# One change to a memory-learning, attention and expert kernel: first weights filled by GpSimd, unused TensorE products in its waits, the last step formed as a mean

## Chip, cores and metric

The kernel runs on one core of one Trainium2 chip, as one program in a single launch. The metric is its device time in microseconds (us), the median of three runs. A profiled execution of the same program gives the rows below. TensorE, VectorE, ScalarE, GpSimd and SyncE stand in the profile as PE (PEld for its weight loads), DVE, ACT, POOL and SP.

## What is computed

Input x is 4 x 32 x 32 x 128 in float32: 4 batches, 32 steps, 32 rows of 128 features. Three layers follow each other, each with a residual sum:

```python
# 1. a small two-block MLP (W1 128x256, W2 256x128, twice) learns per batch by momentum over 32 steps
k, v = l2norm(x_t @ Wk), x_t @ Wv                  # x group-normalised
g = grad(mean((mlp(params, k) - v)**2))            # per batch
mom = eta * mom - lr * g                           # eta, lr, forget: per batch and step
params = params * (1 - forget) + mom
final = mean over the batches of params            # after the last step
x = x + mlp(final, l2norm(x @ Wq))
# 2. banded additive attention over 1024 tokens (32 keys each): tanh(q + k), softmax, weighted sum
# 3. eight experts, the best two per token: softmax router, layernorm, gelu MLP 128-512-128
```

Only the mean of the learned weights is read after the last step, not the weights of each batch.

## The kernel before

The program is five blocks, one after another, each with an instruction stream per engine written out by hand and semaphores between them; at a block's end all engines meet.

- `prepare` loads and normalises x, projects it (8 steps at a time, `CH`), and leaves the normalised keys (`ktok`, and turned `kf`), the scaled values `vs`, the turned queries `qf` and the gates `coef`. VectorE's L255 writes the normalised input `xg`; every projection on TensorE (L180) waits for all four parts. At its end VectorE (L287) and GpSimd (L219) each scale half of `vs`, behind GpSimd's last difference (L216), and VectorE copies the last two blocks of turned queries (L260). ScalarE's queue issues the loads of the first weights (`first10` to `first21`, L94 and L96, semaphore `load_p`); ScalarE waits for them at its end.
- `learn` is the 32 steps. W, M (momentum) and KW (kept part of W) are tiles of 128 x (4 batches x 256) for each of the four weights "10", "20", "11", "21"; WT are turned copies of W. The loop is rotated (`rotated`): a forward for step 0, then 31 turns of backward(t) and forward(t), then backward and the rest of step 31. Ahead of it ScalarE (L528) and VectorE (L630) copy the first weights four times each, and GpSimd clears M (L448) before it copies the coefficients of step 0 (L405). In a step ScalarE makes KW (L483, `keep_of`), the Gelus (L456) and copies out of PSUM; TensorE makes each gradient per batch (`grad_1`, `grad_2`, L669 and L676) into four PSUM banks; VectorE folds them into M (L541, `momentum`); GpSimd (L384, `add`) and for "20" VectorE (L550) sum KW and M to the new W. Layer 10's gradient comes last, behind L579 of the step. SyncE fills the expert rows in HBM by DMA (L372, L373), behind three small fills (`pad_ready`).
- `read_out` reduces W over the batches on VectorE (L959, then L961), in the order 10, 20, 11, 21, and runs the MLP over 8 tiles of 512 tokens: TensorE L905, L915, L925, L935, ScalarE the Gelus, VectorE the sums, statistics and the normalisation `xl` (L966), which waits for `rstd` from GpSimd (`root`, L840 and L842). GpSimd's stream has the conversion of the eight experts' weights into two bfloat16 parts first (L850 to L856), with root(0) ahead of the last one and root(1) behind them.
- `attend` sums and squashes query and key bands (VectorE L1060, ScalarE L1087), sums over units on TensorE, and makes the first softmax. Its last TensorE work is 8 turns (L1127); VectorE's softmax of the first two tiles runs behind it.
- `experts` starts with the routing: for 8 token tiles TensorE turns the attention weights (`weights`, L1378) and applies them (`values`, L1386 and L1388). For each group of two tiles (four groups, `GR`) VectorE normalises (L1540), `router` turns the tokens (L1399) and makes the logits (L1405), VectorE picks two experts, `counts` (L1412, L1413) ranks them, VectorE writes `place` (L1592), and GpSimd sends 16 scatters of rows to HBM (L1361). When all have landed SyncE loads the rows of each job (39 jobs of 256 rows), TensorE turns (L1434) and multiplies them (L1461, L1476), and the results are scattered, gathered and summed (L1702).

The order inside an engine is the order of the code, for instance TensorE's in the routing:

```python
                for n in range(2):
                    weights(n)
                    values(n)
                for g in range(GR):
                    if 2 * g + 2 < NTB:
                        weights(2 * g + 2)
                        values(2 * g + 2)
                    router(g)
                    if 2 * g + 3 < NTB:
                        weights(2 * g + 3)
                        values(2 * g + 3)
                    counts(g)
```

## Time and profile before

| | |
|---|---|
| three runs | 984.9, 987.91, 993.33 us; median 987.91 |
| the profiled execution | 990.18 us, its span 988.3 |
| mean granted TensorE clock | 0.884 of full |
| busy in the span | PE 790.3 us, DVE 731.2, ACT 617.9, POOL 615.3 |
| stages (us from the span's start) | prepare to 72, learning to 575, read-out to 654, attention to 709, routing to 828, experts to 960, sum of the results to the end |

The page shows the span in 40 slices of 24.7 us, with the busy tenths of each engine and the granted clock (9 is 90% or more, 5 is half). A timeline row is start, length, engine, line, operation, output and inputs; several alike in a row are merged (x8), the bracket tells how long the engine had been idle and who released it. The length of one product on TensorE has its drain in it; the distance of two starts is what it costs in a stream.

### The profile page before, as it was taken

The numbers are of one execution on the slowest core, as the hardware profiler recorded it, in microseconds if no ns is written. First come the engines' busy times: TensorE is split into PE (matmuls) and PEld (weight loads), VectorE is DVE, ScalarE is ACT, GpSimd is POOL, SyncE is SP. The second block draws the span as 40 slices with busy tenths as digits, with TensorE's granted clock in tenths as the row PEclk, the third lists the DMA queues.
The fourth block names the chain that finished last, engine by engine and source line by source line (L and its number), as shares of the span: only waits on it lengthen the run. The fifth ranks groups of instructions, "written<-read, shape, count | busy, mean of one in ns | idle before, by whom it ended". The sixth has DMA issues, their size and how long they took to land. (4 is left out here: it accounts for less than half of the span.)

```text
span 988.3 us, 24782 instructions
## 1 busy us (share of the span) xinstructions
PE 790.3 (80%) x7837; PEld 501.2 (51%) x7837; DVE 731.2 (74%) x1853; ACT 617.9 (63%) x1382; POOL 615.3 (62%) x759
## 2 busy tenths in 40 slices
PE   2957999999999999999999969946565522999960
PEld 2544555555555555555555524421254421899950
DVE  4485888888888888888888852759677770777747
ACT  3756877777778777777787713239533421888840
POOL 0145878878788788787887859710006774466660
PEclk8988999999999999999999969968855555999985
DMA  7009999990000000000000032032001112233318
GB/s 231 1 2 206 160 202 147 10 5 0 0 0 0 0 0 0 0 0 0 0 0 0 1 87 86 0 102 89 2 1 43 50 52 57 75 90 91 95 50 254
DMA packets 105404, 54.07 MB, mean 55 GB/s; under 512 B 42624, under 2 KB 96664, under 8 KB 105360
## 3 DMA queue, kind: packets, MB, share of 16 engines
q1 hardware_dynamic: 98976, 43.34, 27.8%
q0 software_dynamic: 4544, 9.38, 2.9%
q10 hardware_dynamic: 1840, 0.79, 0.3%
q8 instruction: 24, 0.39, 0.2%
q14 instruction: 20, 0.16, 0.1%
HBM read 21.49 MB, written 29.44 MB: 52 GB/s over the span
## 5 line engine op out<-in xcount | busy, mean ns | idle before, releaser
L384 POOL TENSOR_TENSOR s_w<-l_kw,l_m 128x512 f32<-128x512 f32 x192 | 260.0, 1355 | 15.4 <-DVE l_m L541 9.9
L541 DVE SCALAR_TENSOR_TENSOR l_m<-l_m,l_eta,lp_g 128x256 f32<-128x256 f32 x512 | 225.0, 477 | 26.5 <-PE lp_g L676 20.2
L483 ACT ACTIVATE l_kw<-s_w,l_keep_lr 128x256 f32<-128x256 f32 x384 | 173.7, 505 | 19.1 <-POOL l_keep_lr L405 19.1
L1366 POOL DMA_INDIRECT f_yg<-f_yr,f_xmeta x78 | 78.4, 1005 | 54.5 <-DVE f_yr L1696 41.7
L1361 POOL DMA_INDIRECT f_xg<-f_xrow,f_place x64 | 63.0, 985 | 54.8 <-DVE f_place L1592 36.2
L389 POOL TENSOR_TENSOR l_kw<-s_w,l_keep 128x512 f32<-128x512 f32 x64 | 71.9, 1124 | 0.0
L1341 ACT ACTIVATE f_hh<-fp_v,f_bcol 128x256 f32<-128x256 f32 x156 | 61.2, 476 | 13.1 <-PE fp_v L1461 9.3
L477 ACT COPY l_wt<-lp_b 128x512 f32<-128x512 f32 x96 | 56.4, 588 | 15.5 <-PE lp_b L662 15.5
L662 PE MATMUL lp_b<-s_cst,s_w 128*128 128x128 f32 x384 | 62.2, 285 | 0.7 <-ACT s_w L528 0.7
L1461 PE MATMUL fp_v<-f_xf,s_w_hi 128*128 128x256 bf16 x312 | 54.6, 277 | 2.3 <-DVE f_xmeta L1676 1.9
L650 PE MATMUL lp_h<-s_w,l_gf 128*32 128x128 f32 x1024 | 41.7, 280 | 18.2 <-ACT l_gf L470 18.2
L662 PEld LDWEIGHTS lp_b<-s_cst,s_w 128*128 128x128 f32 x384 | 43.3, 142 | 24.3 <-DVE l_gp L573 13.2
L550 DVE TENSOR_TENSOR s_w<-l_kw,l_m 128x512 f32<-128x512 f32 x64 | 49.5, 773 | 1.2
L1687 DVE TENSOR_TENSOR f_hs_lo<-f_hh,f_hs_hi 128x512 bf16<-128x512 f32 x52 | 33.6, 689 | 21.4 <-ACT f_hs_hi L1347 21.4
L676 PE MATMUL lp_g<-l_dh,l_g 32*128 32x128 f32 x512 | 45.7, 296 | 0.0
L669 PE MATMUL lp_g<-l_da,l_h 32*128 32x256 f32 x256 | 44.9, 427 | 0.0
L1060 DVE TENSOR_TENSOR t_h<-s_qp,s_kp 128x1056 f32<-128x1056 f32 x32 | 37.5, 1255 | 9.9 <-ACT s_kp L1083 9.9
L216 POOL TENSOR_TENSOR proj<-s_ktok,proj 128x1024 f32<-128x1024 f32 x4 | 8.8, 2191 | 55.6 <-DVE s_ktok L276 55.6
L650 PEld LDWEIGHTS lp_h<-s_w,l_gf 128*32 128x32 f32 x1024 | 25.3, 110 | 35.5 <-issue 25.3
L1461 PE MATMUL fp_v<-f_xf,s_w_lo 128*128 128x256 bf16 x156 | 43.2, 277 | 0.0
L676 PEld LDWEIGHTS lp_g<-l_dh,l_g 32*128 32x128 f32 x512 | 33.5, 185 | 16.8 <-DVE l_m L541 12.3
L662 PE MATMUL lp_a<-s_cst,s_w 128*128 128x128 f32 x256 | 42.0, 287 | 0.0
(320 smaller groups left out, 2029.8 us busy)
## 6 DMA issues: line engine op xcount, KB each, us to landing
f_xg<-s_pad SPq DMA_DIRECT2D x1, 17280.0 KB, 107.8
f_xt<-f_xg SPq DMA_DIRECT2D x39, 130.0 KB
r_w<-in_L_ffn_W_dram SPq DMA_DIRECT2D x16, 256.0 KB, 3.2
s_w<-f_yg SPq DMA_DIRECT2D x16, 256.0 KB, 3.7
xs<-in_x_dram SPq DMA_DIRECT2D x4, 512.0 KB, 6.8
t_w<-in_L_ffn_W_dram SPq DMA_DIRECT2D x8, 256.0 KB
out_dram<-s_x SPq DMA_DIRECT2D x8, 256.0 KB, 3.1
s_xsh<-s_xl SPq DMA_DIRECT2D x4, 448.0 KB, 3.5
```

The source lines that it names most:

```text
L384: nc.gpsimd.tensor_tensor(W[k][:, half(h), :], KW[k][:, half(h), :], M[k][:, half(h), :], ALU.add).then_inc(w_ready[k], 1)
L389: nc.gpsimd.tensor_tensor(KW[k][:, half(h), :], W[k][:, half(h), :], keep[:, half(h)].rearrange("p (b a) -> p b a", a=1).to_broadcast([128 ...
L477: nc.scalar.copy(flat(WT[k][:, half(h), :]), wt_bank(k, h)).then_inc(wt_ready, 1)
L483: m = nc.scalar.mul(KW[k][:, b, :], W[k][:, b, :], keep_lr[:, b:b + 1])
L541: i = nc.vector.scalar_tensor_tensor(out=M[k][:, b, :], in0=M[k][:, b, :], scalar=eta[:, b:b + 1], in1=ps_g[b][:, 0:256], op0=ALU.mult, op ...
L650: i = nc.tensor.matmul(p[rows(b), 0:128], x[:, 128 * h + 32 * b:128 * h + 32 * b + 32], w[:, b, 128 * h:128 * h + 128], start=h == 0, stop ...
L662: i = nc.tensor.transpose(wt_bank(k, h)[:, 128 * j:128 * j + 128], W[k][:, 2 * h + j // 2, 128 * (j % 2):128 * (j % 2) + 128], ident)
L676: i = nc.tensor.matmul(ps_g[b][:, 128 * h:128 * h + 128], x[rows(b), 128 * h:128 * h + 128], y[rows(b), :], start=True, stop=True)
L1341: nc.scalar.activation(hh[j % 2][:, h, :], ps_h[j % 2][:, SL * h:SL * h + SL], ACT.Gelu, bias=bcol[:, h, j:j + 1]).then_inc(h_ready, 1)
L1361: nc.gpsimd.indirect_dma_start(sb["xg"][:, :], bass.IndirectOffsetOnAxis(ap=place[:, g, k, i:i + 1], axis=0), row[k][:, tile_of(g, i), :], ...
L1366: nc.gpsimd.indirect_dma_start(sb["yg"][:, :], bass.IndirectOffsetOnAxis(ap=xmeta[:, j, a, 0:1].bitcast(mybir.dt.int32), axis=0), yr[j % R ...
L1461: m = nc.tensor.matmul(p, chosen(w1s[b], e, h), xf[j % 2][:, c, :], start=r == 0, stop=r == 2)
```

## The change

First, the weights of the first step are filled by GpSimd in `prepare`, when `load_p` has come. The value product is cut at 24 of 32 steps between VectorE and ScalarE (GpSimd has none), and ScalarE copies the last block of turned queries. GpSimd's clearing of M and the two fills for SyncE's DMA stand behind the first forward.

```diff
@@ prepare
+                act.wait_ge(coef_ready, 1)
+                act.wait_ge(k_pad_v, NCK + 1)
+                for t in range(T - CH, T):
+                    nc.scalar.mul(sb["vs"][:, t, :], proj[:, t, 256:384], sb["coef"][:, t, 8:9])
+                act.wait_ge(qk_turned, 4 * NCK - 1)
+                nc.scalar.copy(q_block(2 * NCK - 1), ps[5][:, :].rearrange("p (t b c) -> p t b c", t=4, b=B))
...
+                pool.wait_ge(load_p, 16 * 4)
+                for k in PARAMS:
+                    nc.gpsimd.tensor_copy(sb["w" + k][:, :, :], sb["first" + k][:, :].rearrange("p (a n) -> p a n", a=1).to_broadcast([128, B, 256]))
...
-                pool.wait_ge(k_pad_v, NCK + 1)
-                pool.wait_ge(coef_ready, 1)
-                nc.gpsimd.tensor_tensor(sb["vs"][:, T // 2:T, :], proj[:, T // 2:T, 256:384], sb["coef"][:, T // 2:T, 8:9].to_broadcast([128, T // 2, 128]), ALU.mult)
...
-                dve.wait_ge(k_pad_v, NCK + 1)
-
-                nc.vector.tensor_tensor(sb["vs"][:, 0:T // 2, :], proj[:, 0:T // 2, 256:384], sb["coef"][:, 0:T // 2, 8:9].to_broadcast([128, T // 2, 128]), ALU.mult)
-                for g in range(2 * NCK - 2, 2 * NCK):
-                    q_turned(g)
+                dve.wait_ge(k_pad_v, NCK)
+                nc.vector.tensor_tensor(sb["vs"][:, 0:T - CH, :], proj[:, 0:T - CH, 256:384], sb["coef"][:, 0:T - CH, 8:9].to_broadcast([128, T - CH, 128]), ALU.mult)
+                q_turned(2 * NCK - 2)
```

GpSimd's stream from prepare to the loop of learning, before (`s_kf` keys, `l_m` M, `l_kw` KW, `l_keep_lr` coefficients, `s_padrow` the fill for the DMA):

```order
L212 MEMSET s_kf 128x128
L216 ISA
L216 TENSOR_TENSOR proj<-s_ktok,proj 128x8x128 x4
L219 TENSOR_TENSOR s_vs<-proj,s_coef 128x2048
L76 UNCONDITIONAL_BRANCH
L375 UNCONDITIONAL_BRANCH
L442 MEMSET l_none 128x4
L443 MEMSET s_padrow 128x270
L444 IOTA s_padrow 128x270
L445 COPY l_kt<-s_kf 128x128
L448 MEMSET l_m 128x512 x8
L405 COPY l_keep_lr<-s_coef 128x5
```

And now, where M lies in `s_w_mem` and KW in `s_xsh` (the rows from L80 to L456 are in learning):

```order
L231 COPY s_w<-s_first 128x1024 x4
L235 ISA
L235 TENSOR_TENSOR proj<-s_ktok,proj 128x8x128 x4
L80 UNCONDITIONAL_BRANCH
L389 UNCONDITIONAL_BRANCH
L459 MEMSET l_none 128x1 x4
L418 COPY l_keep_lr<-s_coef 128x5
L420 TENSOR_TENSOR l_keep<-l_keep_lr,l_none 128x4
```

Four copies of 1024 elements stand ahead of the first difference, the product of L219 is gone, and the eight fills (now L454) come behind eight further instructions of the first forward.

Second, the last step has functions of its own (`last`). Gradients are made for the sum of the batches, in one product over all 128 rows, where `grad_1` and `grad_2` made one for each batch; no W is formed. For "10" the sum over the batches of eta M + KW and the gradient are added in one PSUM bank, and ScalarE scales it; for the others VectorE adds the gradient to batch 0's decayed M, and `read_out` sums M and KW over the batches:

```diff
@@ learn
+                def total(t, k, n):
...
+                    nc.vector.scalar_tensor_tensor(out=M[k][:, 0, :], in0=M[k][:, 0, :], scalar=eta[:, 0:1],
+                                                   in1=ps_g[n - 1][:, 0:256], op0=ALU.mult, op1=ALU.add).then_inc(decayed_ready, 1)
...
+                    total(t, "21", 1)
+                    slope_times(t, 1, ps_a, DG1)
+                    decayed(t, "10", (0, 1))
+                    decayed(t, "10", (2, 3))
+                    dve.wait_ge(mm_done, t * 7 + DH1)
+                    nc.vector.tensor_tensor(dh1[:, :], ps_h[:, 0:128], dp[:, :], ALU.add).then_inc(chain, 1)
...
+                    act.wait_ge(grad_done, t * 6 + 4)
+                    nc.scalar.mul(sb["wf"]["10"][:, :], ps_g[3][:, 0:256], 1.0 / B)
...
+                    pe.wait_ge(decayed_ready, 5)
+                    for b in range(B):
+                        nc.tensor.matmul(ps_g[3][:, 0:256], ident, M["10"][:, b, :], start=b == 0, stop=False)
+                    pe.wait_ge(kc_ready, t + 1)
+                    pe.wait_ge(chain, t * 6 + K_DA0)
+                    total_1(ps_g[3], kc, da[0], start=False)
@@ read_out
+                    if e == 0:
+                        pool.wait_ge(wf_ready, len(PARAMS) - 1)
...
+                n = mean(0, "20", ())
+                n = mean(n, "11", (1, 2, 3))
+                mean(n, "21", (1, 2, 3))
```

TensorE's end of learning, from the product with the turned "11" on, before (`lp_g` gradient banks, `l_dh` and `l_da` the errors, `l_kc` the keys):

```order
L650 MATMUL lp_h<-l_wt,l_daf 32x128 x8
L669 MATMUL lp_g<-l_da,l_h 128x256 x2
L656 MATMUL lp_t<-s_cst,l_dh 128x128
L676 MATMUL lp_g<-l_dh,l_g 128x128 x4
L642 MATMUL lp_b<-l_wt,l_dh1f 32x256 x4
L676 MATMUL lp_g<-l_dh,l_g 128x128 x4
L669 MATMUL lp_g<-l_da,l_kc 128x256 x4
```

And now:

```order
L707 MATMUL lp_h<-l_wt,l_daf 32x128 x8
L713 MATMUL lp_t<-s_cst,l_dh 128x128
L818 MATMUL lp_g<-l_dh,l_g 128x128 x2
L699 MATMUL lp_b<-l_wt,l_dh1f 32x256 x4
L851 MATMUL lp_g<-s_w_mem,s_cst 128x256 x4
L813 MATMUL lp_g<-l_da,l_kc 128x256
```

The gradients by batch are one or two products each, and four with the identity (`s_cst`) stand ahead of the last. M, KW and eta now outlive `learn`: they lie in the space of `w2_both` and `xsh`.

Third, products whose result nobody reads: 3 and 2 in `prepare` (float32, 384 columns), 26 at the end of `attend`, and in `experts` 4 ahead of each values' wait, 5 and 3 in `router`, 8 ahead of the wait in `counts`, 4 and then 16 ahead of a group, 76 ahead of turn(0) (bfloat16, 384 columns):

```diff
+def unused(nc, sb, p, n):
+
+    w = sb["w1_hi"]
+    for _ in range(n):
+        nc.tensor.matmul(p[:, 0:384], w[:, 0, 0:128], w[:, 1, 0:384], start=True, stop=True)
@@ experts
                 def values(n):
+                    unused(nc, sb, ps_xn, 4)
                     pe.wait_ge(at_ready, n + 1)
...
                 m.then_inc(table_done, 1)
+                unused(nc, sb, ps_am, 76)
                 turn(0)
```

TensorE's stream of group 0, from its first router work to the ranks, before (`fp_x`, `fp_y`, `fp_v` PSUM, `f_xn` tokens, `f_am` attention weights):

```order
L1399 MATMUL fp_x<-s_cst,f_xn 128x128 x8
L1405 MATMUL fp_y<-f_wr,f_xnf 128x8 x8
L1378 MATMUL fp_y<-s_cst,f_am 128x128 x4
L1379 MATMUL fp_x<-s_cst,f_tail 128x128
L1386 MATMUL fp_v<-s_xsh,f_at 128x128 x4
L1388 MATMUL fp_v<-s_xtail,f_at 128x128 x4
L1412 MATMUL fp_y<-f_both,s_cst 128x64
```

And now:

```order
L1118 MATMUL fp_y<-s_w_hi 128x384 x5
L1521 MATMUL fp_x<-s_cst,f_xn 128x128 x4
L1118 MATMUL fp_y<-s_w_hi 128x384 x3
L1521 MATMUL fp_x<-s_cst,f_xn 128x128 x4
L1527 MATMUL fp_y<-f_wr,f_xnf 128x8 x8
L1496 MATMUL fp_y<-s_cst,f_am 128x128 x4
L1497 MATMUL fp_x<-s_cst,f_tail 128x128
L1118 MATMUL fp_x<-s_w_hi 128x384 x4
L1505 MATMUL fp_v<-s_xsh,f_at 128x128 x4
L1507 MATMUL fp_v<-s_xtail,f_at 128x128 x4
L1118 MATMUL fp_y<-s_w_hi 128x384 x8
L1535 MATMUL fp_y<-f_both,s_cst 128x64
```

Nothing of the real work has moved; L1118 stands in front of what waits.

## Rows read from the trace of the kernel before

**Rows 1.** The page's 40 slices: the granted clock, in tenths of full.

```profile
PEclk8988999999999999999999969968855555999985
```

**Rows 2.** Timeline of the start of learning, and the same Gelus in the loop.

```profile
72.69 1.28 ACT L524 ACT_TABLE_LOAD   x1 [4.09 <-PEq L76]
...
73.74 4.63 POOL L448 MEMSET l_m<- 128x512 f32 x8
...
79.01 0.36 ACT L456 ACTIVATE l_g<-lp_a 128x256 f32<-128x256 f32 x1
...
84.58 0.38 ACT L456 ACTIVATE l_g<-lp_b 128x256 f32<-128x256 f32 x1
...
554.50 0.38 ACT L456 ACTIVATE l_g<-lp_a 128x256 f32<-128x256 f32 x1 [0.78 <-PE lp_a L689]
...
558.82 0.38 ACT L456 ACTIVATE l_g<-lp_b 128x256 f32<-128x256 f32 x1
```

**Rows 3.** Timeline of the end of prepare.

```profile
65.42 3.64 POOL L219 TENSOR_TENSOR s_vs<-proj,s_coef 128x2048 f32<-128x2048 f32 x1
...
65.45 5.76 DVE L287 TENSOR_TENSOR s_vs<-proj,s_coef 128x2048 f32<-128x2048 f32 x1 [1.47 <-POOL proj L216]
...
71.13 1.27 DVE L260 COPY s_qf<-pp 128x512 f32<-128x512 f32 x2
```

**Rows 4.** Timeline of the last step and the start of the read-out.

```profile
566.89 0.64 PE L642 MATMUL lp_b<-l_wt,l_dh1f 128*32 128x256 f32 x8
...
572.18 2.48 POOL L384 TENSOR_TENSOR s_w<-l_kw,l_m 128x512 f32<-128x512 f32 x2 [2.13 <-DVE l_m L541]
...
577.28 3.78 PE L905 MATMUL rp_a<-s_qf,r_wf 128*128 128x512 f32 x4 [6.24 <-DVE r_wf L961]
...
590.95 1.88 PE L925 MATMUL rp_a<-r_h,r_wf 128*128 128x512 f32 x4
```

**Rows 5.** GpSimd's timeline: the first scatters of groups 0, 1 and 2.

```profile
743.11 1.29 POOL L1361 DMA_INDIRECT f_xg<-f_xrow,f_place  x1 [32.91 <-DVE f_place L1592]
...
764.87 0.96 POOL L1361 DMA_INDIRECT f_xg<-f_xrow,f_place  x1 [1.02 <-DVE f_place L1592]
...
787.42 0.95 POOL L1361 DMA_INDIRECT f_xg<-f_xrow,f_place  x1 [2.29 <-DVE f_place L1592]
```

**Rows 6.** The tile of the first weights (its loads, all landings), then VectorE's timeline.

```profile
L96 ACTq DMA_DIRECT2D s_first<-in_L_conv_w_dram x2: 468/482/497, 6.4 to 6.9; - x2
DMA to landing us min/median/max: 13.4/13.9/14.5
...
21.79 2.98 DVE L255 TENSOR_SCALAR xg<-s_vs,grs,gneg 128x1024 f32<-128x1024 f32 x4
```

**Rows 7.** Timeline of the read-out: GpSimd's root(1) and its user.

```profile
629.19 1.04 POOL L842 TENSOR_TENSOR r_rstd<-r_ve,r_mhalf 128x4 f32<-128x4 f32 x1
...
631.71 1.91 DVE L966 TENSOR_SCALAR s_xl<-s_x,s_mv,r_rstd 128x128 f32<-128x128 f32 x4
```

**Rows 8.** The chain at the start of the experts' products.

```profile
834.96 1.47 PE fp_v L1461 x6
...
844.88 1.31 PE fp_v L1461 x12
```

**Rows 9.** Windows: length, busy (x) of PE, PEld, DVE, ACT, POOL, clock, DMA, GB/s.

```profile
690.00:700.00 10.00, 5.53 (x36) 1.25 (x36) 9.73 (x9) 9.01 (x10) 0.00 (x0) 1.00 0.00 0
710.00:720.00 10.00, 6.90 (x33) 5.65 (x34) 8.50 (x28) 2.35 (x5) 0.20 (x1) 0.50 0.04 6
743.10:764.90 21.80, 14.62 (x70) 12.27 (x70) 15.80 (x71) 8.51 (x12) 16.21 (x17) 0.50 0.15 49
```

**Rows 10.** The chain from 709.6 to 743.2, then TensorE's timeline at 723.

```profile
by line: PE fp_v L1386 12.4%; PE fp_y L1405 9.6%; PE fp_y L1378 9.2%; DVE f_am L1501 7.7%; PE fp_x L1399 6.7%; DVE f_xn L1540 5.8%; ACT f_xrow L1316 5.3%; ACT f_at L1293 5.2%; PE fp_v L1388 4.5%; issue 3.7%; ACT L1320 3.4%; DVE f_bst L1512 
718.50 2.08 PE fp_v L1386 x8
...
723.35 1.16 PE L1386 MATMUL fp_v<-s_xsh,f_at 128*128 128x128 f32 x8 [0.84 <-ACT f_at L1294]
```

345 lines of the change are left out of this document (212 added, 133 removed).

## Prediction

> **What bounds the kernel now.** I read the page's slices first, then the timeline at the places that the diff touches, then windows, the chain and GpSimd's own timeline in the routing. In the slices [rows 1] TensorE's granted clock is at half (5, of its two levels of 2.4 and 1.2 GHz the lower) around slice 28 to 33, at about 0.8 twice before that, and at full elsewhere. The 31 turns of the learning loop in the middle have the same instructions in both kernels (only addresses and buffers differ), so I put their change at 0 and look at six seams.
>
> At the start of learning [rows 2] the Gelu of step 0 begins at 79.01, 6.32 us after the block's first instruction at 72.69: ScalarE's first kept weights wait for the coefficients that GpSimd copies behind 4.63 us of memsets. From that Gelu to the second one takes 5.57 us (79.01 to 84.58), in the loop 4.32 (554.50 to 558.82), though the loop also does gradients there: TensorE starts at half clock. At the end of prepare [rows 3] VectorE's product of 2048 elements shows 5.76 us. GpSimd's equal product ran from 65.42 to 69.06, and VectorE ended at 71.21, 2.15 us later, which is what 2048 elements cost it. So it stood still while GpSimd had the memory, and both must end before learning begins. At the end of learning [rows 4] the last backward product is done at 567.5, but GpSimd's last sums of weights end at 574.66 and the first product of the read-out starts at 577.28, at half clock. In the routing GpSimd scatters rows in 4 groups of 16; it starts each group when VectorE has placed it, and once going it idles only 1.02 and 2.29 us before groups 1 and 2 [rows 5].
>
> **The change part by part.** *Weights filled in prepare.* GpSimd copies four tiles of 1024 elements. A copy isn't in the trace; its memset takes 4.63/8 = 0.58 per 512 elements [rows 2], its sum with two inputs 1.24 [rows 4], so one tile costs 1.2 to 2.5, and I take 1.2 (one input, like the memset), 4.6 in all. They wait for the loads issued at 6.4 to 6.9, which land 13.4 to 14.5 later, so they begin at about 20.5, and VectorE makes the normalised input at 21.79 to 24.77, all of which TensorE waits for [rows 6]. If VectorE stands still as at 65.45, the copies left at 21.8 (3.3 us) stand in front or between. Some of VectorE's small steps before fall beside them, so +2.8; bounds 0 and +4.8 (all four, none beside).
> The Trainium skill says the same of such pairs ("SBUF — State Buffer", Who interferes with whom): a VectorE copy or tensor_scalar in a two-port mode, or an instruction with two inputs in SBUF, and a reading GpSimd instruction shut each other out for the whole instruction. Row 65.45 agrees with it (3.6 us of standstill). By the rule 4.8 is the most it could cost, without it the term would be 0 and the sum 2.8 lower.
>
> *End of prepare.* The value product is cut anew: VectorE does 24 steps (3072 elements, 3.2 us by 2.15 for 2048) and GpSimd none, ScalarE does 8 small ones and one turned block. VectorE no longer waits for GpSimd's last difference but can't run beside it, which ended at 65.45 [rows 3]: 65.45 + 3.2 + one copy of 0.64 = 69.3, against 71.13 + 1.27 = 72.4: -3.1. ScalarE's new eight of some 0.2 to 0.4 us (estimated from the 0.36 of its 256-element Gelu in [rows 2]) and the copy follow its last turned keys and end at about 69 to 70.5. The unused products keep the clock there. I take -3.0, bounds 0 and -4.
>
> *Start of learning.* The copies of weights (8 on ScalarE, 8 on VectorE) and the copy of the keys are gone, and GpSimd's memsets stand behind its first pass. Gelu then waits for ScalarE alone: table load 1.28, a one-column Gelu 0.2, one kept product 0.45: 1.95 instead of 6.32, -4.4. With at most a microsecond or two between TensorE's unused products and its first real ones, it starts at full clock: -1.2 (5.57 to 4.32). The memsets now end about 9.2 us into the block, and TensorE's first gradient product of the loop waits for them at about 9.0: +0.3. The two fills for SyncE's DMA stand behind them; that DMA is wanted at 743 only. Together -5.3, bounds -4 and -6.5.
>
> *Last step.* Gradients are summed over the batches in one product; GpSimd has nothing. VectorE's decayed momenta of layer 10 now stand ahead of its next chain step and wait for ScalarE's kept products: some 0.7 late, so the last backward product ends at about 568.2. Then TensorE does four 256-column sums with the identity and one gradient. Two 512-column products are 4 records and 1.88 in all, 0.43 apart (at 590.95) [rows 4], so one of 256 columns is 0.43, five 2.2, with the drain 570.6, and ScalarE's scaling 0.4: 570.9. The block ends 3.7 earlier than by 574.66. The first read-out product needs nothing more: it starts at about 571.4, not 577.28, and after less than 1 us of idle at full clock, so the first two steps take 1.88, not 3.78 each: at the first product of layer 11 (590.95 before) TensorE is 9.1 ahead. VectorE's three means take 8.2 us from the block's start and are there when wanted.
> But GpSimd converts expert weights from the block's start in both, and normalising tile group 1 waits for a root that it makes behind them. Before, that root was done at 630.23 and used at 631.71 [rows 7], 1.5 of slack. It moves by 3.7 only, so at this point the gain is 3.7 + 1.5 = 5.2. VectorE then finds TensorE's products waiting and catches up about 1.1 in the tail: -6.3. Bounds: -3.7 (block alone) and -9.1 (TensorE alone).
>
> *Attention.* Its body is VectorE's and unchanged. In its last idle stretch 26 unused products of 384 columns run: 12 of 256 take 1.31 at full clock [rows 8], 0.109 each, so 0.164 here, 4.3 in all. Beside them VectorE does the softmax of the first tiles, some 4 us too, so what can reach past the block's end is a little: +0.1, bounds 0 and 0.5 (4 if the clock were at half).
>
> *Routing.* In this stage the clock is 0.50 though TensorE is busy 14.62 of 21.8 us per group, while attention holds it at 1.00 with 5.53 of 10 [rows 9]. The same 8 value products take 2.08 at one level and 1.16 at the other [rows 10]. If the fill keeps the level, the real work of a group is about 7.5 and its 40 unused products (4+4, 5+3, 8, 16) are 6.6: 14 of 20, so they fit in waits. What it buys: up to the first normalised tokens VectorE sets the pace (8.50 of 10 busy), so 0.8 of the 1.5 idle. Behind them the turns of the tokens (L1399, 6.7% of the chain's 33.6 us) and the router's products (L1405, 9.6%) stand on the chain [rows 10], 5.5, half saved, 2.7; a cast of ScalarE's takes back 0.3 and I take 2.5. The first scatter so starts 3.3 earlier than 743.11. From there GpSimd sets the end: 64 scatters of 1.26. A group's period falls from 21.8 to about 19, below its 20.2, so of faster groups only the two idles count, 1.02 + 2.29 less the usual 0.3 each: 2.7. Sum -6.0; if nothing comes of it 0, and at most -9 (if the value products and turns before the first normalised tokens, L1386, L1388 and half of L1378 or 7.2 us, save their half too).
>
> *Start of experts.* The 76 unused products end before the first rows land (12.5 at full clock, up to 25 at half, from about 806) and may leave an idle stretch in which the clock falls again. At full clock the first 6 products take 0.7 instead of 1.47, and from 844.88 on the stage is already at full [rows 8]. -0.4, between 0 and -0.9.
>
> Sum: +2.8 - 3.0 - 5.3 - 6.3 + 0.1 - 6.0 - 0.4 = -18.1. The profiled execution took 990.18, so 972.1; it is 2.3 above the median of the three runs shown (987.91), by which it would be 969.8. I take 971.
>
> **The rivals.** *The unused products become the bound (slower).* For it: the clock stayed at half in the routing at 67% busy. At half a product of 384 columns costs 0.33, 40 of them 13.1, and 14.62 + 13.1 = 27.7 is more than the 21.8 of a group. Groups 1 and 2 then slip by 5.9 and 5.3, the first and last by about 6 together, and the scatters end 16 later; the 76 in front of the first turned rows (25 us) add some 9. +25 against -11.7 elsewhere: 990.2 + 13 = 1003, with the median's offset 1001. It decides once the routing loses more than 12. Against it: TensorE would then be busy all the time with wide products, and such stretches are at full level everywhere else. 5%.
> *The fill holds no clock but fits, and the routing gains nothing.* GpSimd's 64 scatters then start at 743.1 as before: -12 in all, 976. 12%.
> *GpSimd holds both ends.* The copies cost 4.8 and the read-out gains only the 3.7 of the block: +2.0 and +2.6 on the sum, -13.5: 975. 15%. With the rival before: 980 to 981, 8%.
> *It doesn't do what it says.* If the last step's sums cost as much as the old path (VectorE's decays blocking the chain), the seam gives 0 and the sum is -11.8: 976. 5%.
>
> **How the numbers follow.** The forecast has 55%, the rivals 5, 12, 15, 8 and 5. Three runs of the kernel before spread from 984.9 to 993.33, and about 1% (9.9 us) is what tells it from no change: faster is below 978. The forecast, the two cases at 975 and 976 and most of the last give 0.82; the double case and tails of the others 0.13; the half-clock case 0.05. The range reaches from 961 (every term at its good end but one) to 983.
>
> **What would show it.** Right: Gelu of step 0 about 2 us after its block starts; no GpSimd work in the last step, the first read-out product 6 us earlier in its stage and at 1.88; clock 1.00 through 710 to 800, the first scatter some 3 us nearer to the routing's start, scatters without gaps. Wrong: VectorE's normalised input no longer than 2.98 near 21.8; slices of 0.5 in the routing, or TensorE never idle there; gaps between scatter groups; or a loop turn of other length, which times 31 would upset everything.

## The result, and the profile after

The changed kernel takes 974.69 us (median of 4: 972.06, 972.13, 977.25, 977.40), the kernel before, run beside it, 986.72 (984.90 to 993.33). The ratio is 0.9853, with an interval of 0.9821 to 0.9885: faster by about 1.5%. The forecast was 971 with a range of 961 to 983. Its profiled execution took 972.06 with a span of 970.2, against 990.18 and 988.3: 18.1 less, the sum of the forecast, though not by its terms in every place. The two profiled executions flatter the change: the one before lies 3.5 above its median and the one after 2.6 below its own, so the medians differ by 12.0 only. The four times lie in two pairs 5.2 apart, and the profile shows one of the lower pair. The experiments find two things that such a spread can come from; no trace shows the upper pair itself.

From the page of the changed kernel, the granted clock in 40 slices of 24.3 us, in tenths of full:

```profile
PEclk8899999999999999999999999967999867999985
```

The five half-clock slices of [rows 1] (717 to 840 us) are gone. What is left is at the end of the read-out and the attention's start (6, 7), and in the later part of the routing and in front of the experts (8, 6, 7). Windows of 10 us have 1.00 from 670 to 750, then 0.83, 0.95 and 0.84, and from 780 on:

```profile
780.00:790.00 10.00, 0.00 (x0) 0.00 (x0) 9.24 (x26) 0.00 (x0) 7.56 (x9) 0.50 0.14 47
790.00:800.00 10.00, 8.94 (x43) 4.83 (x44) 1.20 (x3) 0.00 (x0) 7.56 (x9) 0.68 0.17 55
```

A row of windows gives the length, then for PE, PEld, DVE, ACT and POOL the busy time and the number of instructions, then the granted clock, the DMA share and GB/s. TensorE's last product of the routing starts at 778.29, so up to 806 the half clock behind it hits only the 76 unused products.

Timeline of VectorE and GpSimd at the first weights, after (start us, busy us, engine, line, operation, and in brackets the idle time before it with what ended it):

```profile
21.10 4.90 POOL L231 COPY s_w<-s_first 128x1024 f32<-128x1024 f32 x4 [20.16 <-DMA s_first<-in_L_conv_w_dram]
...
22.19 5.08 DVE L271 TENSOR_SCALAR xg<-s_vs,grs,gneg 128x1024 f32<-128x1024 f32 x4
```

It answers to [rows 6]: VectorE's four instructions grew from 2.98 to 5.08, and even the four small ones ahead of them (0.16 in all) took 0.60. The first projection product moved from 24.83 to 27.33.

Timeline of the end of prepare and the start of learning, after:

```profile
66.44 4.55 DVE L302 TENSOR_TENSOR s_vs<-proj,s_coef 128x3072 f32<-128x3072 f32 x1
70.92 0.68 DVE L276 COPY s_qf<-pp 128x512 f32<-128x512 f32 x1
...
72.18 1.28 ACT L558 ACT_TABLE_LOAD   x1 [0.25 <-PEq L80]
...
74.12 0.36 ACT L468 ACTIVATE l_g<-lp_a 128x256 f32<-128x256 f32 x1
...
79.36 0.38 ACT L468 ACTIVATE l_g<-lp_b 128x256 f32<-128x256 f32 x1 [0.46 <-PE lp_b L699]
```

Against [rows 2, 3] the table load stands 0.5 earlier although 2.5 were lost in front of it, so the end of prepare gave 3.0. The first Gelu follows 1.94 behind the load instead of 6.32; from it to the second one are 5.24, not the 4.3 of full clock.

Timeline of VectorE and TensorE in the last step and the read-out's start, after:

```profile
558.55 0.88 DVE L658 SCALAR_TENSOR_TENSOR s_w_mem<-s_w_mem,s_eta,s_xsh 128x256 f32<-128x256 f32 x2 [0.76 <-ACT s_xsh L495]
559.35 0.28 DVE L682 TENSOR_TENSOR l_dh<-lp_h,l_dp 128x128 f32<-128x128 f32 x1
...
560.97 1.99 PE L851 MATMUL lp_g<-s_w_mem,s_cst 128*128 128x256 f32 x8
...
564.11 1.96 PE L1001 MATMUL rp_a<-s_qf,s_first 128*128 128x512 f32 x4 [0.72 <-PEq L379]
```

The last forward's second Gelu is at 551.92 (558.82 before [rows 2]), so all in front of it gave 6.9. From there to the first read-out product are 12.19 instead of 18.46 [rows 4], and that product is at full clock.

GpSimd's timeline, a window of the routing of one scatter group's length, and the chain in front of the experts, after:

```profile
725.35 1.29 POOL L1479 DMA_INDIRECT f_xg<-f_xrow,f_place  x1 [28.76 <-DVE f_place L1719]
```

```profile
725.35:746.00 20.65, 15.23 (x115) 10.90 (x116) 17.61 (x76) 8.41 (x12) 15.92 (x16) 1.00 0.15 50
```

```profile
815.40 1.47 PE fp_v L1588 x6
```

The last of the 64 scatters is at 807.56, and none behind the first waited for VectorE, where [rows 5] show two that did. The window is at 1.00 with 115 instructions of TensorE where [rows 9] has 0.50 with 70. The experts' first six products are still at half, 1.47 as in [rows 8].

| stretch | before | after |
|---|---|---|
| to the first projection product | 24.83 | 27.33 |
| to the table load of learning | 47.86 | 44.85 |
| to the second Gelu of step 0 | 11.89 | 7.18 |
| to the same Gelu of step 1 | 17.02 | 15.25 |
| to the same Gelu of step 31 | 457.22 | 457.31 |
| to the read-out's first product | 18.46 | 12.19 |
| to the attention's first product | 77.69 | 77.47 |
| to the first scatter | 88.14 | 83.77 |
| to the last scatter | 83.97 | 82.21 |
| to the first result scatter | 19.97 | 19.94 |
| to the last result scatter | 112.96 | 113.02 |
| to the end of the span | 28.29 | 29.68 |

The table follows the span from mark to mark, in one execution of each kernel ("the same Gelu" is the second Gelu of that step). The experiments are read by it, since a mark in a profile is surer than a few microseconds in a median. Three seams come out nearly alike in all fourteen traces of this study: from the table load to the first Gelu are 6.32 and 6.31 in the kernel before and e2, and 1.94 in the other twelve; from the last step's second Gelu to the read-out's first product are 18.46 and 18.47 in those two and 11.34 to 12.19 in the others; and from the first projection product to the table load 47.86 and 47.69 against 44.5 to 45.8. No experiment takes these three parts of the change out again.

### The profile page after: what moved, and what is told of

Its sections match the earlier page's. It is cut to its first block and busy times, and to the rows that moved or that the text cites. A ratio compares the mean times of both kernels' runs of the same rounds, so it can differ in the third digit from the quotient of the medians.

```text
span 970.2 us, 25223 instructions
## 1 busy us (share of the span) xinstructions
PE 811.6 (84%) x8069; PEld 506.3 (52%) x8069; DVE 722.1 (74%) x1846; ACT 618.1 (64%) x1384; POOL 608.7 (63%) x758
## 3 DMA queue, kind: packets, MB, share of 16 engines
q1 hardware_dynamic: 98976, 43.34, 28.9%
## 5 line engine op out<-in xcount | busy, mean ns | idle before, releaser
L398 POOL TENSOR_TENSOR s_w<-s_xsh,s_w_mem 128x512 f32<-128x512 f32 x186 | 251.8, 1354 | 8.9 <-DVE s_w_mem L570 3.4
L570 DVE SCALAR_TENSOR_TENSOR s_w_mem<-s_w_mem,s_eta,lp_g 128x256 f32<-128x256 f32 x496 | 217.8, 475 | 24.0 <-PE lp_g L733 18.6
L495 ACT ACTIVATE s_xsh<-s_w,l_keep_lr 128x256 f32<-128x256 f32 x384 | 173.8, 505 | 17.5 <-POOL l_keep_lr L418 17.4
L403 POOL TENSOR_TENSOR s_xsh<-s_w,l_keep 128x512 f32<-128x512 f32 x64 | 72.1, 1126 | 0.0
L1459 ACT ACTIVATE f_hh<-fp_v,f_bcol 128x256 f32<-128x256 f32 x156 | 61.1, 476 | 13.1 <-DVE f_hs_lo L1814 5.6
L579 DVE TENSOR_TENSOR s_w<-s_xsh,s_w_mem 128x512 f32<-128x512 f32 x62 | 48.0, 775 | 1.1
L489 ACT COPY l_wt<-lp_a 128x512 f32<-128x512 f32 x64 | 37.7, 589 | 6.8 <-PE lp_a L719 6.8
```

Of the source, the lines that this page charges most:

```text
L398: nc.gpsimd.tensor_tensor(W[k][:, half(h), :], KW[k][:, half(h), :], M[k][:, half(h), :], ALU.add).then_inc(w_ready[k], 1)
L403: nc.gpsimd.tensor_tensor(KW[k][:, half(h), :], W[k][:, half(h), :], keep[:, half(h)].rearrange("p (b a) -> p b a", a=1).to_broadcast([128 ...
L489: nc.scalar.copy(flat(WT[k][:, half(h), :]), wt_bank(k, h)).then_inc(wt_ready, 1)
L495: m = nc.scalar.mul(KW[k][:, b, :], W[k][:, b, :], keep_lr[:, b:b + 1])
L570: i = nc.vector.scalar_tensor_tensor(out=M[k][:, b, :], in0=M[k][:, b, :], scalar=eta[:, b:b + 1], in1=ps_g[b][:, 0:256], op0=ALU.mult, op ...
L1459: nc.scalar.activation(hh[j % 2][:, h, :], ps_h[j % 2][:, SL * h:SL * h + SL], ACT.Gelu, bias=bcol[:, h, j:j + 1]).then_inc(h_ready, 1)
```

## The experiments

Twelve kernels were made for it. Times are medians, and ratios are to the kernel before, run beside each. "Course" is one of two lengths that the same rows of instructions took.

### e1: no unused products behind learning

```diff
 def unused(nc, sb, p, n):
-    w = sb["w1_hi"]
-    for _ in range(n):
-        nc.tensor.matmul(p[:, 0:384], w[:, 0, 0:128], w[:, 1, 0:384], start=True, stop=True)
+    return
```

> The changed kernel without its unused products behind the attention, in the routing and in front of the experts; those in prepare stay. In the changed kernel the first scatter starts 83.97 us after the attention's first product (641.38 to 725.35) and the last one 82.21 behind the first; before it was 88.49 and 83.97. Theory (the fill holds TensorE's clock, and that is the whole of the routing's gain): the clock is at half again in the routing, the two stretches come back to 88.5 and 84.0, and the profiled execution takes 6.3 more than 972.1, so 978.4. Rival (the gain comes from the earlier seams shifting the stage, not from the clock): 84.0 and 82.2 stay, 972. In front of the experts nothing changes by either, since the first products there ran at half clock with the fill too.

980.43 us (976.41 to 981.61), ratio 0.9906 (0.9878 to 0.9934): 5.7 more than the changed kernel, 5.2 by the ratios. A window of one scatter group and GpSimd's scatters, the first and those that waited:

```profile
732.60:754.00 21.40, 14.62 (x70) 12.27 (x70) 15.47 (x69) 8.51 (x12) 16.15 (x16) 0.50 0.15 49
```

```profile
732.59 1.29 POOL L1477 DMA_INDIRECT f_xg<-f_xrow,f_place  x1 [32.41 <-DVE f_place L1717]
...
754.34 0.96 POOL L1477 DMA_INDIRECT f_xg<-f_xrow,f_place  x1 [1.02 <-DVE f_place L1717]
...
776.89 0.96 POOL L1477 DMA_INDIRECT f_xg<-f_xrow,f_place  x1 [2.28 <-DVE f_place L1717]
```

The window at 0.50, the 14.62 busy and both waits of before [rows 5, 9] are back within 0.01. (The attention's first product is at 641.58 and 654.97; the 641.38 of this expectation, and in e4's the 77.27, come from a row of SyncE's just ahead of it, so 83.97 and 88.49 are 83.77 and 88.14.) From the attention's first product to the first scatter are 87.59, and 84.21 to the last. From VectorE's first sum of the attention to the last scatter are 164.84, as in the kernel before (164.89), and 159.42 in the changed kernel. The rival (earlier stages shift this one) falls, and the fill is the gain, through the clock. In front of the experts, 19.91 instead of 19.94 without the 76: they buy nothing. The read-out took 80.57 instead of 77.47 here, though nothing in it was changed; see e5.

### e2: the kernel before with the unused products alone

The edit is the diff's own lines in the attention and the routing, except the 76.

> The kernel before with only the unused products added: 26 behind the attention, 4+4, 5+3, 8 and 16 per group in the routing; none in prepare, none in front of the experts. Theory (the fill works alone): attention's first product to first scatter 84.0 instead of 88.49, first to last scatter 82.2 instead of 83.97, all else as before: 990.2 - 6.3 = 983.9 for a profile like the one of before, ratio 0.994. Rival (the fill pays only together with the other edits, or costs where TensorE is late): less than 3 us of it, ratio 0.997 or above.

984.64 us, ratio 0.9957 (0.9939 to 0.9975): 4.2 less than before. The profile has 82.09 for the scatters as expected, but 86.65 in front of them, and in this execution the fill gave 2.0 in all (162.89 from the attention's first sum to the last scatter). The fill works alone, and gives 4 rather than 6 in the median. Its span, 987.6, also holds a first turn of the loop of 19.21: the stop of 1.38 that the kernel before has there too, and behind it the clock at 0.50 from 98 to 104.

### e3: copies of the first weights later

```diff
                 pool.wait_ge(load_p, 16 * 4)
+                pool.wait_ge(xg_ready, B)
                 for k in PARAMS:
```

> The changed kernel with GpSimd's four copies of the first weights behind VectorE's normalised input instead of beside it. Theory (the two engines shut each other out of the memory): VectorE's four instructions take 2.98 again instead of 5.08, the first projection product moves from 27.33 to about 24.9, and everything behind it by as much: -2.4, 969.7 for the profiled execution. Rival (the lengthening has another cause, such as the loads from DRAM landing then, or the later copies hit the next VectorE work, the norms from some 32 on, as hard): less than 1 us.

971.96 us (970.45 to 975.41), ratio 0.9846 (0.9812 to 0.9880). VectorE's and GpSimd's timelines:

```profile
21.87 2.98 DVE L272 TENSOR_SCALAR xg<-s_vs,grs,gneg 128x1024 f32<-128x1024 f32 x4
...
25.01 3.98 POOL L232 COPY s_w<-s_first 128x1024 f32<-128x1024 f32 x4 [24.06 <-DVE xg L272]
...
34.69 2.29 DVE L283 TENSOR_REDUCE ss<-xs 128x16 f32<-128x2048 f32 x1 [9.84 <-ACT xs L128]
```

2.98 again, the projection at 24.91 and the table load at 69.43 instead of 72.18. Apart, both engines are shorter (3.98 against 4.90 for the copies), and VectorE idles 9.84 behind them anyway. The times of whole runs can't tell 2.4 here; the marks can.

### e4: GpSimd's first two roots earlier

```diff
-                    if e == E - 1:
-                        root(0)
...
                     nc.gpsimd.tensor_copy(sb["w1_hi"][:, e, :], w1g[e % 2][:, :]).then_inc(w_hi, 1)
+                    if e >= E - 2:
+                        root(e - (E - 2))
...
-                root(1)
```

> The changed kernel with GpSimd's first root inside the last expert but one and its second inside the last expert, each ahead of the two subtractions. In the changed kernel VectorE idles 2.48 and 2.56 for them (611.96 and 619.37). Theory (GpSimd holds the read-out from the first normalised group on): both idles shrink below 0.5, the attention's first product comes some 2 to 3 us sooner after the read-out's first one than 77.47 (564.11 to 641.38 is 77.27), 969.5 in all. Rival (TensorE's own row of products is as long, so that it takes the place of the root): under 0.7 us.

971.18 us (968.96 to 972.47), ratio 0.9833 (0.9805 to 0.9861). VectorE's three first normalisings in the changed kernel and in e4:

```profile
611.96 1.69 DVE L1076 TENSOR_SCALAR s_xl<-s_x,s_mv,r_rstd 128x128 f32<-128x128 f32 x4 [2.48 <-POOL r_rstd L937]
...
619.37 2.07 DVE L1076 TENSOR_SCALAR s_xl<-s_x,s_mv,r_rstd 128x128 f32<-128x128 f32 x4 [2.56 <-POOL r_rstd L937]
...
623.74 1.08 DVE L1076 TENSOR_SCALAR s_xl<-s_x,s_mv,r_rstd 128x128 f32<-128x128 f32 x4
```

```profile
610.18 3.22 DVE L1075 TENSOR_SCALAR s_xl<-s_x,s_mv,r_rstd 128x128 f32<-128x128 f32 x4
...
616.48 2.77 DVE L1075 TENSOR_SCALAR s_xl<-s_x,s_mv,r_rstd 128x128 f32<-128x128 f32 x4
...
623.79 1.12 DVE L1075 TENSOR_SCALAR s_xl<-s_x,s_mv,r_rstd 128x128 f32<-128x128 f32 x4 [2.00 <-POOL r_rstd L937]
```

Both waits are gone, but the read-out shortened by 1.4 only (76.07). Counted from its first product, the first group begins 2.4 earlier and ends 0.8 earlier, since the same instructions take 3.22 instead of 1.69 beside GpSimd's subtractions; the second ends 2.8 earlier; and the third begins only 0.5 earlier, because it now waits 2.00 for the third root, which stands behind the clears. So GpSimd held the read-out by three things in turn: its order, its work beside VectorE's, and the clears.

### e5: SyncE's large DMA early again

```diff
                 for k in PARAMS:
                     pool.wait_ge(w_ready[k], 2)
+                nc.gpsimd.memset(sb["padrow"][:, :, 1:2], 0).then_inc(pad_ready, 1)
+                nc.gpsimd.iota(sb["padrow"][:, :, 0:1], ...).then_inc(pad_ready, 1)
                 rotated(pool, forward, backward, lambda t: None, cleared)
```

The same two lines are taken out behind the memsets of the momenta.

> The changed kernel with the two fills that SyncE's large DMA into the sorted rows waits for put ahead of the first step, as early as before, instead of behind the eight memsets. In the kernel before, the loop's first turn (second Gelu to second Gelu) takes 17.02 instead of 15.24, with a row of 1.38 in which TensorE waited for nothing that the profile shows (95.58); in the changed kernel it takes 15.25. Theory (the DMA moving at some 280 GB/s from 75 on delays the first pass through the loop's code): the first turn is 17 or more again, the DMA seen from about 74. Rival (it is only which execution was caught, or the shorter forward of the first step): 15.25 to 15.6.

978.26 us (one run). TensorE's timeline, in the loop's first turn:

```profile
89.39 0.41 PE L699 MATMUL lp_b<-l_wt,l_dh1f 128*32 128x256 f32 x2 [0.74 <-issue]
```

The DMA moves some 270 to 290 GB/s from 74.5 on, as in the kernel before, and the first turn takes 16.58: 1.33 of the 1.77 are back, 0.74 of them in a stop of TensorE for nothing that the profile shows. In the changed kernel and the ten others of this study with the DMA behind the memsets that turn took 15.24 to 15.65. So one run puts it between the theory (17 or more) and its rival (15.6 at most), nearer to the theory. The DMA by itself isn't enough: in the changed kernel it is issued at 81.21 instead of 73.52 and moves 258 to 284 GB/s from 82 to 92, within the same turn (79.36 to 94.61). The turn is longer only in the traces where it began well before. Why is not shown; that what was late is the loop's code is a guess.

The same profile shows a second course of the read-out. VectorE and TensorE around 621, e5:

```profile
620.84 3.35 DVE L1076 TENSOR_SCALAR s_xl<-s_x,s_mv,r_rstd 128x128 f32<-128x128 f32 x4 [2.58 <-POOL r_rstd L937]
```

```profile
624.25 0.66 PE L1048 MATMUL rp_t<-s_cst,s_xl 128*128 128x128 f32 x4 [2.85 <-DVE s_xl L1076]
624.74 2.98 PE L1021 MATMUL rp_a<-r_h,s_first 128*128 128x512 f32 x4
```

Where the changed kernel's profile has 2.07 and an idle TensorE of 1.54, this has 3.35 and 2.85, then half clock for 4 us, and the read-out takes 80.57 instead of 77.47. GpSimd clears the attention's buffers at that moment (two clears of 1.14 and 1.11 in the changed kernel, 1.01 and 0.98 in e5). The instructions are the same; where VectorE takes longer GpSimd takes less, so which engine gets through first differs. Every kernel with these lines shows one of the two: 2.07 in the changed one, e3, e6 and e10 (77.44 to 77.55), 3.35 in e1, e5, e7 and e8 (80.38 to 80.57; e8 has its own edit there). That would be 3.1 of the 5.2 between the pairs, if the upper pair had this course; no trace of it tells.

The Trainium skill ("SBUF — State Buffer", Who interferes with whom) says that VectorE in a two-port mode and GpSimd lock each other out for a whole instruction, and that the first to issue gets the ports. The rows agree: in the changed kernel and e5 the same four instructions take 1.08 where GpSimd idles or works on 4 elements per partition, and 1.69 to 3.35 beside its instructions on 512 and more.

### e6: no unused products in prepare

```diff
-                unused(3)
                 pe.wait_ge(sig_ready, 1)
...
-                unused(2)
```

> The changed kernel without the 3+2 unused products at the end of prepare. Theory (they hold the clock up to the first products of learning): table load where it was (72.2 to 72.8), the first pass from first to second Gelu 5.57 as before instead of 5.24, so +0.3 and not more, since with them too the clock was at half from 75.5 to 79.4. Rival (they also speed up the last turns and dots of prepare): the table load comes 0.5 or more later. Second rival (they cost where they stand): the table load comes earlier.

974.74 us (one run). Table load at 73.11, first to second Gelu 5.92. With the products the traces of this study give 72.07 to 73.11 and 4.91 to 5.93, so neither number tells anything: what those five products are worth stays open, within about the microsecond by which those traces differ among themselves.

### e7: the chain step first, and a longer tail

```diff
                     decayed(t, "10", (0, 1))
-                    decayed(t, "10", (2, 3))
                     dve.wait_ge(mm_done, t * 7 + DH1)
                     nc.vector.tensor_tensor(dh1[:, :], ps_h[:, 0:128], dp[:, :], ALU.add).then_inc(chain, 1)
+                    decayed(t, "10", (2, 3))
...
-                unused(nc, sb, ps_am, 76)
+                unused(nc, sb, ps_am, 118)
```

> Two edits at seams that don't touch each other. In the last step VectorE's decayed momenta of batches 2 and 3 of layer 10 stand behind the chain step instead of ahead of it: theory (they hold it up by 0.6, since they wait for ScalarE's kept products): second Gelu of the last step to first read-out product 11.6 instead of 12.19; rival (the identity sums then wait for them, the last to be formed): 12.2 or more. In front of the experts 118 unused products instead of 76, which should end where the first rows land: theory of the forecast (full clock for the first expert products): last scatter to first result scatter 19.94 becomes 19.0 to 19.5; rival (the first tile's later steps on the other engines set it): 19.9; if the clock is at half for longer than thought, they end later than the rows and it becomes more than 20.

980.54 us (one run). In the last step 11.35 instead of 12.19: the two decays had cost 0.84. In front of the experts (TensorE's timeline):

```profile
801.41 0.29 PE L1573 MATMUL fp_y<-f_mine,s_btab 128*128 128x39 bf16 x4 [12.31 <-DVE s_btab L1788]
801.54 21.57 PE L1118 MATMUL fp_y<-s_w_hi 128*128 128x384 bf16 x118
822.94 0.61 PE L1560 MATMUL fp_x<-f_identb,f_xt 128*128 128x128 bf16 x8
```

They begin after 12.31 of idle, at half clock, and last 21.57 instead of the 19.4 of full clock (118 times the forecast's 0.164, an estimate). In the other traces the first turned rows follow the last scatter by 5.5 to 5.8 (807.56 to 813.21 in the changed kernel), so here the rows would have been there at about 818.2, and the 118 end some 4.8 too late. The first result scatter came 4.0 later (23.98), not 4.8: the first expert products ran at full clock and the second rows had landed meanwhile, and how the 0.7 divides between the two isn't separated. This is the forecast's slower rival in small: filling that runs past its wait.

### e8: unused products in the read-out's tail

```diff
                         n = k - 7
+                        if k >= N + 3:
+                            pe.wait_ge(w_hi, 4)
+                            unused(nc, sb, ps_a0, {N + 3: 8, N + 4: 12, N + 5: 9, N + 6: 7}[k])
...
+                unused(nc, sb, ps[0], 7)
                 pe.wait_ge(load, 16 * 7)
```

> The changed kernel with 36 more unused products in TensorE's waits in the last four turns of the read-out and 7 more ahead of the attention's first product. In the changed kernel the clock falls to half around 632 and the attention's four groups of products take 5.9 (641.58 to 647.46), the first three turns 1.11 instead of 0.66. Theory (filled waits hold the level here as in the routing): clock 1.00 from 620 to 650, the four groups some 3.5, VectorE's first sum of the attention (648.14) 2.5 to 3.5 sooner after the read-out's first product than 84.03. Rival (the products delay the turns they stand in front of, or the clock falls all the same, as it did in the read-out's tail in every trace so far): less than 0.5.

973.60 us (970.29 to 976.58), ratio 0.9856 (0.9806 to 0.9906). TensorE's timeline at the attention's start:

```profile
642.63 1.30 PE L863 MATMUL rp_a<-s_w_hi 128*128 128x384 bf16 x7
643.76 0.62 PE L1058 MATMUL rp_t<-s_cst,s_xl 128*128 128x128 f32 x4
645.31 1.30 PE L863 MATMUL tp<-s_w_hi 128*128 128x384 bf16 x7 [0.93 <-PEq L903]
646.53 1.06 PE L1225 MATMUL tp<-s_qf,s_wt 128*32 128x512 f32 x8
```

This execution had the 3.35 of e5 and so starts 3.1 behind. From 630 to 652 the clock is at full, and a group of the attention's products takes 1.06 instead of 1.94. But the seven in front of the attention's first product begin with its block, at 645.31, and hold it up to 646.53, 1.2 later than it could begin. The seven ahead of the read-out's last turn cost nothing that shows: VectorE's last normalised tile is ready at 643.66, the turn starts at 643.76. The first sum of the attention comes 86.59 behind the read-out's first product, beside 86.48 to 87.53 in e1, e5 and e7: half a microsecond, where 2.5 to 3.5 was expected. Here the half clock behind the 3.35 also lasted longer: the two rows of four that follow the late turn span 6.2, in e5 5.3. The mechanism is right, and one of its five places was wrong.

### e9: roots and clears out of each other's way

As e4, and:

```diff
                 nc.gpsimd.memset(sb["rst"][:, :, 0:1], 0.0).then_inc(cleared, 1)
+                for b in (sb["wa"][:, :], sb["wag"][:, :, :], sb["xtail"][:, S // 128 - 1, :], sb["qp"][:, :], sb["kp"][:, :]):
+                    nc.gpsimd.memset(b, 0.0).then_inc(sb["attn_cleared"], 1)
                 pool.wait_ge(col_in, 32 * E)
...
+                nc.gpsimd.memset(sb["xsh"][:, :, 0, :], 0.0).then_inc(sb["attn_cleared"], 1)
                 root(2)
```

Where these clears stood before, they are taken out.

> The changed kernel with GpSimd's first two roots inside the last two experts, as in e4, and its four clears of the attention's buffers at the start of the read-out, where GpSimd idles 8.01 for a load, instead of between the second root and the third. Theory (the two run times of the changed kernel, near 972 and 977, come from one place: VectorE's normalising of tile group 1 takes 2.07 in one and 3.35 in the other beside those clears, and in the second TensorE idles 2.85, falls to half clock and the read-out takes 3.1 more): the three normalised groups wait no more than 0.5 for a root, read-out's first product to attention's first product 74.0 to 75.0 instead of 77.5 or 80.5, no fall of the clock around 620 to 626, and the times of the runs no longer in two groups. Rival (two groups come from elsewhere, as from the routing's clock, 77.0 to 80.8 from the attention's first sum to the first scatter in the traces so far): the runs still spread over 5.

974.12 us (969.01, then 973.72 to 974.76), ratio 0.9839 (0.9808 to 0.9870). No normalising waits for a root before the last group, and the read-out takes 75.12. Yet the times still spread over 5.8, so a spread of that size needs no second course of the read-out: the rival is right. GpSimd's scatters that waited, and two windows of the routing:

```profile
747.92 0.96 POOL L1478 DMA_INDIRECT f_xg<-f_xrow,f_place  x1 [1.41 <-DVE f_place L1718]
...
771.27 0.96 POOL L1478 DMA_INDIRECT f_xg<-f_xrow,f_place  x1 [3.17 <-DVE f_place L1718]
```

```profile
710.00:720.00 10.00, 8.92 (x48) 7.68 (x48) 6.86 (x29) 4.53 (x6) 0.00 (x0) 0.66 0.00 0
730.00:740.00 10.00, 8.14 (x39) 6.51 (x38) 6.84 (x26) 2.58 (x4) 7.71 (x8) 0.65 0.16 53
```

The clock falls several times in spite of the 40 products per group, and GpSimd then waits longer than before the change. From the attention's first sum of VectorE to the last scatter the traces give:

| unused products per group | traces | us |
|---|---|---|
| 0 | before, e1 | 164.89, 164.84 |
| 40 | after, e2 to e9, e11 | 158.91 to 164.75, mean of ten 161.3 |
| 80 | e10, e12 | 160.16, 160.38 |

The routing's instructions are the same in the ten, one execution each. So the fill is worth 3.5 in the mean, and anything from 0 to 6 in one execution.

### e10: twice the fill

Each number of unused products in the routing is doubled (8, 10 + 6, 16, 32).

> The changed kernel with twice the unused products in the routing: 80 per group instead of 40, 13.1 at full clock beside 7.5 of real work in a group of 19 to 20. Theory (at 40 they fit in waits and at 80 they don't): the stage gets slower by 1 to 3 per group from first to third, last scatter 4 to 8 later against the attention's first sum than 159.4, 976 to 980 in all; TensorE is then busy all the time, and the clock never falls before the last group. Rival (more of them hold the clock better, and VectorE and GpSimd still set the end): attention's first sum to last scatter 158 to 160, 972 or less. Rival 2, the slower one of the forecast (they become the bound at half clock): 15 later and more.

974.94 us (971.42 to 977.21), ratio 0.9867 (0.9835 to 0.9900). A window:

```profile
720.00:730.00 10.00, 10.00 (x73) 6.62 (x72) 7.53 (x37) 2.58 (x4) 2.02 (x2) 1.00 0.03 8
```

TensorE is hardly idle and the clock is 1.00 from 670 to 780, and the stage takes 160.16, neither 4 to 8 more nor less than the best with 40. The theory added 13.1 of unused products to 7.5 of real work, 20.6 in a group of 20, and took a full TensorE for a slower stage. It wasn't: 80 cost nothing that can be seen. The forecast's slower rival needed half clock, which TensorE did not have in this trace while the 80 ran.

### e11: everything that helped, in one

Besides e3, e9 and e7's first part:

```diff
-                unused(2)
+                unused(4)
...
+                    if not grads:
+                        for _ in range(2):
+                            nc.tensor.matmul(ps_g[0][:, 0:256], ident, W["21"][:, 0, :], start=True, stop=True)
                     pe.wait_ge(gelu_ready, t * 2 + 1)
...
+                        if k >= N + 3:
+                            pe.wait_ge(w_hi, 4)
+                            unused(nc, sb, ps_a0, {N + 3: 7, N + 4: 9, N + 5: 6, N + 6: 3}[k])
```

> The changed kernel with e3's later copies, e7's order in the last step, e9's roots and clears, 2 more unused products at the end of prepare and 2 sums with the identity in learning's first forward step while it waits for Gelu, and in the last four turns of the read-out 7, 9, 6 and 3 unused products, none in front of the attention. Each seam by itself: copies -2.4; first to second Gelu 5.24 to 4.4, -0.8; last step -0.8; read-out -3.0; attention's first products at full clock, -2.0. Sum -9.0: 963 for the profiled execution, ratio to before 0.974 to 0.978. Where one eats another (the clock falls elsewhere, earlier stages hand their gain to a wait): 966 to 968.

962.93 us (961.34 to 963.98), ratio 0.9743 (0.9722 to 0.9763): faster than both the kernel before and the changed one. TensorE's timeline in learning's first step and at the attention's start, then the page's slices:

```profile
71.81 1.03 PE L753 MATMUL lp_g<-s_w,s_cst 128*128 128x256 f32 x4
73.07 0.44 PE L714 MATMUL lp_t<-s_cst,l_g 128*128 128x128 f32 x2 [0.23 <-ACT l_g L469]
...
633.36 0.66 PE L1061 MATMUL rp_t<-s_cst,s_xl 128*128 128x128 f32 x4 [0.44 <-DVE s_xl L1089]
635.09 1.07 PE L1227 MATMUL tp<-s_qf,s_wt 128*32 128x512 f32 x8 [1.08 <-PEq L907]
```

```profile
PEclk8899999999999999999999999989999768999985
```

With two products in the wait for Gelu and two more at the end of prepare (TensorE idles 0.49 between the blocks instead of 1.77) the first step is at full clock: 4.27 instead of 5.24. The read-out takes 74.39, and from the attention's first product to VectorE's first sum are 4.32 instead of 6.56. The second Gelu of step 0 is 2.4 earlier (only that, for the block starts at 70.71, not the 69.43 of e3), the last step 0.9, the read-out 3.1, the attention's products 2.2, the way to the last scatter 0.5, and the rest, nearly all of it behind the last result scatter, 1: 10.2 of span.

### e12: the same with twice the fill

The edit is e11's with e10's numbers, and the 76 products in front of the experts are taken out.

> e11 with twice the unused products in the routing (80 per group), as in e10, and without the 76 in front of the experts, without which e1's last scatter to first result scatter took 19.91 against 19.94 with them. Theory (with 40 per group the clock still falls for some microseconds in the routing, at another place in each execution; with 80 it doesn't, and they still fit): clock 1.00 from the attention's end to the last scatters, attention's first sum to last scatter 158 to 160.5, 960 to 962, the five runs within 2 of each other. Rival (what 80 gain by the clock they cost in front of the real products, as e10's 160.16 beside 158.91 to 159.5 of the best traces with 40): 962 to 964, no difference from e11's 962.93. Rival 2 (the 76 do hold something for the first expert products): last scatter to first result scatter 20.3 or more.

962.46 us (961.33 to 962.86), ratio 0.9732 (0.9703 to 0.9762). The slices:

```profile
PEclk8899999999999999999999999989999966999985
```

The clock is 1.00 from 700 to 770, and the stage takes 160.38 beside e11's 158.91: no difference from e11 that can be measured, as the first rival said. The five times lie within 1.5, e11's within 2.6. Without the 76 products the first result scatter follows at 19.99 (19.97 in e11), so they are of no use.

## Why the prediction was right

*Weights filled in prepare*, +2.8 (0 to +4.8): +2.5, with its mechanism, and e3 takes it away.

*End of prepare*, -3.0: -3.0. VectorE's product stood still for GpSimd's difference (4.55 for what was put at 3.2) but was free of the wait behind it.

*Start of learning*, -5.3: -4.7. The 4.4 of Gelu's wait is exact. The 1.2 for full clock were 0.33: the step that failed is "with at most a microsecond or two" of idle "it starts at full clock". TensorE idles 1.77 between the blocks and 1.09 for Gelu, and is at half from about 76. e11, which fills both, gets 0.97 back. The 0.3 for the memsets were none.

*The loop*, put at 0: -1.7, all in its first turn. "The same instructions in both" was true; what ran beside them was not the same. Behind the memsets the DMA is issued 7.7 later (81.21 instead of 73.52), and by then that turn was under way. I had written of it only that it is wanted at 743. e5 gives 1.33 of it back.

*Last step*, -6.3: -6.5. Block -3.7 (4.0), decays 0.7 late (0.84 by e7), sums with the identity 2.2 (1.99 the four), TensorE 9.1 ahead at layer 11's first product (9.4), and then GpSimd's root took the rest, as written: VectorE waits 2.56 for it.

*Attention and routing*, -5.9: -6.1 in the profiled execution, of which 5.5 lie behind the attention's first sum; 0.7 is the way to that sum (7.22 to 6.56), where no fill stands. The scatters gave 1.8 of the 2.7 put on them, the way to the first one more than the 3.3. e1 gives 5.4 back. But the mean of ten traces is 3.5 (e2's times: 4.2). "If the fill keeps the level" was the step on which it stood, and it keeps it in part: the place was right and the size was that of a good case. "Clock 1.00 through 710 to 800" held to 750. The rival "gains nothing", at 12%, is in time what e9's profile had.

*Start of experts*, -0.4: 0.0. I had seen that the 76 end before the rows land and might leave an idle stretch; they did, 6.99, and the first six products took 1.47 as in [rows 8]. Whether a fill that ended with the landing would save the 0.4, no run shows: in e7 it ended 4.8 too late and cost 4.0.

*The end*, not in the sum: +1.4 between the last result scatter and the end of the span. The kernel before and the twelve of the experiments have 28.3 to 28.9 there (29.68 in this one execution); no cause is known.

One reading of the rows was off: beside the slices at 0.8 there are two at 0.6 in [rows 1], 568 to 593 and 642 to 667. The second is the read-out's end and the attention's start, which the forecast left alone and where e11 finds 2.2.

That the two profiles differ by 18.1, as forecast, is luck: the loop's 1.7 and the end's 1.4, both unforeseen, nearly cancel, and so do the 1.0 that learning and the start of the experts fell short and the 0.7 that the copies, the last step and the routing did better. What was right is the mechanism of the three largest seams, and the sizes of two of them. The median, 974.7, is 3.7 above the 971 of the forecast, and the 12.0 between the medians are 0.7 of the 16.9 that it had put there (987.91 to 971). Of the 3.7 the routing's mean (3.5 instead of 6.0) would explain 2.5, and the second course of the read-out (3.1) more, where it occurs; that division is argued, not measured. *GpSimd holds both ends* (975, 15%) gives the right number for another reason; its copies cost 2.5, not 4.8, and the read-out gave 6.5.

## What to carry to other kernels

Unused products pay where they leave no idle stretch and end before the real work is ready: 76 that stopped 7 us too early bought nothing, 118 that ran some 5 us too long cost 4.0, seven in front of work that was ready cost 1.2, and a few in the wait itself gave 1.0 in learning and 2.2 at the attention's start. One profile of each kernel is not enough where the granted clock or two engines in each other's way decide: compare marks over several executions, and look for two courses of the same instructions. GpSimd's clears and copies should go where it idles, for a load say, and not beside VectorE's long instructions; here four clears moved and two roots made earlier gave 2.4 on the read-out (e9), and the later copies 2.4 (e3).

## What was not expected

The same rows took two courses: VectorE's four normalising instructions 2.07 or 3.35, and behind them a whole stage 3.1 longer. The loop's first turn was 1.3 to 4.0 longer in the three traces in which a DMA of 17,280 KB, that nobody waits for until much later, had begun well before it (17.02 and 19.21 in the two kernels that had it from 74.5 on, 16.58 in e5, 15.24 to 15.65 in the other eleven); the 19.21 hold a fall of the clock besides. And filling TensorE wholly in the routing (80 products per group) neither helped nor hurt against a good execution with half of them, 160.2 and 160.4 against 158.9 to 159.5: while the clock is at full, the stage no longer depends on how full TensorE is. That VectorE and GpSimd then set it is the likely reason, not a tested one.
